# Slot zero of an eight-slot attention and FFN kernel: VectorE's additions, a low part, and the row sums' way through DRAM in another order

## What is computed

```
xn  = layernorm(x)
t, p, g = Wt @ c,  Wp @ xn,  Wg @ c            # 512x512 by 512x2048
att = sum over a group of p * g                 # 8 groups of 64 channels
y   = group-norm( Wz_grouped @ (att * t) ) * gn_w + gn_b
x1  = x + y + c
x2  = layernorm(x1)
out = x1 + FFN(x2[:, perm]) un-permuted         # 16 heads: 128 -> 512 -> gelu -> 128
```

## Time and profile before

| | |
|---|---|
| median of 3 runs | 1519.7 us (1517.99, 1519.7, 1523.19) |
| span of the profiled execution, first to last instruction | 1516.6 us |
| lowest run, beside that span | 1517.99 us, 1.4 us above it |
| PE busy | 1496.1 us, 99% of the span |
| DVE, ACT, POOL busy | 1192.4, 1065.8, 962.8 us |
| slot zero's S products, y products, v products start at | 5.2, 55.3, 100.6 us |

### The profile page before, as it was taken

The page is one execution under the profiler, slowest core; times in us unless marked ns, Lnnn a source line. Parts: engine busy times, 40 slices in busy tenths (PEclk is TensorE's granted clock), DMA queues, the critical chain, the costliest instruction groups (busy, mean ns, idle before and its releaser), DMA issues.

```text
span 1516.6 us, 19144 instructions
## 1 busy us (share of the span) xinstructions
PE 1496.1 (99%) x6592; PEld 1233.7 (81%) x6592; DVE 1192.4 (79%) x1514; ACT 1065.8 (70%) x1321; POOL 962.8 (63%) x765
## 2 busy tenths in 40 slices
PE   8999999998999999999999999999999999999998
PEld 7878888887888888888888888888888888777886
DVE  4989868875788767887678877888778876889876
ACT  4636757844878568784687847878378773899876
POOL 1673686297862668626784357834579355898887
PEclk9999999999999999999999999999999999999999
DMA  9998788786677936778376784767747776768886
GB/s 327 330 379 332 229 301 298 269 265 204 202 264 266 276 118 221 246 262 278 119 237 248 246 260 133 261 237 250 231 146 275 249 237 204 236 197 257 289 285 221
DMA packets 166865, 374.76 MB, mean 247 GB/s; under 512 B 14960, under 2 KB 80496, under 8 KB 158576
## 3 DMA queue, kind: packets, MB, share of 16 engines
q1 hardware_dynamic: 141424, 281.25, 56.3%
q0 software_dynamic: 25344, 92.29, 17.3%
HBM read 287.45 MB, written 86.03 MB: 246 GB/s over the span
## 4 chain that ended last, share of the span: by engine, by line
PE 80%; DVE 4%; POOL 4%; DMA 4%; ACT 3%; issue 3%; SPq 0%; POOLq 0%; ACTq 0%; DVEq 0%
PE PP L892 13%; PE PP L938 12%; PE PP L953 12%; PE PP L896 6%; PE PP L941 6%; PE PP L957 6%; PE PP L879 6%; PE PP L880 6%; PE PP L874 6%; PE PP L909 4%; PE PP L913 2%; POOL out L1346 1%; POOL FB L1338 1%; POOL FB L1341 1%; ACT Z L1031 1%
## 5 line engine op out<-in xcount | busy, mean ns | idle before, releaser
L938 PE MATMUL PP<-GG,WW 128*128 128x512 f32 x1008 | 270.5, 390 | 4.4 <-issue 4.4
L1046 ACT ACTIVATE PP<-PP 128x1024 f32<-128x1024 f32 x256 | 262.0, 1024 | 0.0
L1249 DVE TENSOR_TENSOR R<-PP,R 128x1024 fp32r<-128x1024 f32 x175 | 213.6, 1220 | 52.5 <-ACT PP L1046 50.6
L892 PE MATMUL PP<-R,WC 128*128 128x512 f32 x1024 | 253.1, 389 | 0.7 <-ACT Z L998 0.7
L1330 POOL TENSOR_TENSOR X<-X,RAW 128x512 f32<-128x512 f32 x112 | 189.2, 1725 | 96.4 <-DVE bn L1069 71.6
L1045 ACT ACTIVATE R<-PP 128x1024 fp32r<-128x1024 f32 x175 | 180.1, 1029 | 87.5 <-PE PP L941 86.5
L938 PEld LDWEIGHTS PP<-GG,WW 128*128 128x128 f32 x1008 | 189.6, 188 | 44.4 <-issue 4.8
L892 PEld LDWEIGHTS PP<-R,WC 128*128 128x128 f32 x1024 | 192.1, 188 | 41.0 <-ACT Z L998 1.1
L1084 DVE TENSOR_TENSOR R<-RAW,R 128x1024 fp32r<-128x1024 f32 x128 | 184.1, 1445 | 49.8 <-ACT R L976 49.8
L1346 POOL DMA_INDIRECT out<-FB,perm_sb x128 | 153.4, 1198 | 82.0 <-DVE FB L1255 64.1
L1323 POOL DMA_INDIRECT FB<-xg_scratch,perm_sb x128 | 127.7, 997 | 115.1 <-DMA xg_scratch<-FB 74.4
(11 more groups left out here) (122 smaller groups left out, 2582.5 us busy)
## 6 DMA issues: line engine op xcount, KB each, us to landing
WW<-w_scratch SPq DMA_DIRECT2D x148, 512.0 KB
X<-in_x SPq DMA_DIRECT2D x32, 1024.0 KB, 6.0
RAW<-in_cx SPq DMA_DIRECT2D x32, 1024.0 KB
RAW<-in_xT SPq DMA_DIRECT2D x63, 512.0 KB
RAW<-in_cT SPq DMA_DIRECT2D x63, 512.0 KB
xg_scratch<-FB SPq DMA_DIRECT2D x104, 256.0 KB
w_scratch<-WW POOLq DMA_DIRECT2D x16, 1024.0 KB, 6.8
HX<-wp_scratch SPq DMA_DIRECT2D x7, 1024.0 KB, 8.2
```

The lines of the kernel that those rows point to most:

```text
L892: eng.matmul(PP[2 + ot // 2][:, ot % 2, :], WC[:, l, ct, part(ot)], u[:, ct, :], start=(l == 0 and ct == 0), stop=False)
L938: eng.matmul(pp[:, e, :], wt[:, l, part(2 * p + e)], g[:, 0, :], start=(l == 0), stop=False)
L1046: eng.activation(pp[:], pp[:], ACT.Gelu).then_inc(S["gelu"], 1)
L1249: eng.tensor_tensor(h_tile(f, p, 1), PP[slot["up", f, p]][:], f32(h_tile(f, p, 0)), ALU.subtract).then_inc(S["hlo"], 1)
```

## The change

It touches the table of numbers in `plan()`, for slot zero (`first`) and at one place slot one, and moves two stages of slot zero from SP's list to ACT's.

```diff
@@ -602,12 +602,12 @@
             put(t + 0.2, s_lo, i, dt)
             for c1 in range(NT):
                 whole = i < 2 or dt > 3
-                put(s0 + (dt + 0.08 * c1 if whole else S_EARLY[c1 // 2][dt][c1 % 2]), s_hh, i, dt, c1)
+                put(s0 + (0.81 if (i, dt, c1) == (1, 0, NT - 1) else dt + 0.08 * c1 if whole else S_EARLY[c1 // 2][dt][c1 % 2]), s_hh, i, dt, c1)
                 put(s0 + (dt + 0.34 + 0.16 * c1 if whole else S_EARLY[c1 // 2][dt][c1 % 2]), s_mm, i, dt, c1)
         for q in range(NQ):
             for ct in range(NT):
                 t = s0 + 6 + 2.1 * ct + 0.4 * q + (1.9 if ct == 3 else 0)
-                t = 10.4 + 1.4 * ct + 0.22 * q if first else s0 + 11 + 2.1 * ct + 0.5 * q if i == 1 else t
+                t = (10.4, 12.65, 14.05, 15.0)[ct] + (0.22 if ct < 3 else 0.15) * q if first else s0 + 11 + 2.1 * ct + 0.5 * q if i == 1 else t
                 put(t, bn_x, i, ct, q)
         if first:
             for ct in range(NT):
@@ -619,14 +619,15 @@
         put(y0 + (12.4 if 0 < i < 3 else 4.2), load_wg, i)
         for q, t in enumerate((y0 - 3, y0 + 0.4, y0 + 4.3, y0 + 8.3)):
             put(t, y_hi, i, q)
-            put(t + 0.2, y_lo, i, q)
+            put(y0 - 0.2 if first and q == 1 else t + 0.2, y_lo, i, q)
         for q, t in enumerate((y0 - 1, y0 + 1.2, y0 + 2.6, y0 + 4.6)):
             for ct in range(NT):
                 put(t + 0.25 * ct + late, row_c, i, q, ct)
-                put(y0 - 1.5 + 2.4 * q + 0.5 * ct + 2 * late, add_c, i, q, ct)
+                tc = (y0 - 2.1, y0 - 2.05, y0 - 1.2, y0 - 0.4)[ct] if q == 0 else y0 + (0.9, 4.6, 6.4)[q - 1] + 0.5 * ct
+                put(tc if first else y0 - 1.5 + 2.4 * q + 0.5 * ct + 2 * late, add_c, i, q, ct)
         put(y0 + 5.8 + late, sum_c, i)
         put(y0 + 5.9 + late, store_sum, i)
-        put(y0 + 7.6 + late, spread_sum, i)
+        put(y0 + (10.5 if first else 7.6 + late), spread_sum, i)
         for c1 in range(NT):
             put(y0 + 11.3 + (0.6 if i < 2 else 0) + 0.6 * c1, s_fix, i, c1)
             put(y0 + 11.5 + (0.6 if i < 2 else 0) + 0.6 * c1, s_evh, i, c1)
@@ -648,9 +649,9 @@
         put(v0 + 3.4, aggr_y, i)
         put(f0 + 1.2, g_mean_mm, i)
         put(f0 + 1.25, g_mean, i)
-        put(f0 + 2.3, g_var_mm, i)
-        put(f0 + 2.35, g_var_a, i)
-        put(f0 + 2.4, g_root, i)
+        put(f0 + (3.3 if first else 2.3), g_var_mm, i)
+        put(f0 + (3.35 if first else 2.35), g_var_a, i)
+        put(f0 + (3.4 if first else 2.4), g_root, i)
         put(f0 + (3.9 if first else 5.25), g_var_b, i)
 
 
@@ -1045,6 +1046,19 @@
                 eng.activation(h_tile(f, p, 0), pp[:], ACT.Gelu).then_inc(S["hhi"], 1)
                 eng.activation(pp[:], pp[:], ACT.Gelu).then_inc(S["gelu"], 1)
 
+            elif stage == "store_sum" and a[0] == 0:
+                i = a[0]
+                act.wait_ge(*at["sst", i, "row"])
+                for r in range(4):
+                    eng.dma_start(vs_d[i].rearrange("(t r j) -> t r j", r=4, j=32)[:, r, :],
+                                  rowc[32 * r:32 * r + NT, :]).then_inc(S["vs"], 16)
+            elif stage == "spread_sum" and a[0] == 0:
+                i = a[0]
+                act.wait_ge(*at["vs", i])
+                for t in free["sb", i]:
+                    act.wait_ge(*t)
+                eng.dma_start(FB[:, SBT, :], vs_d[i].partition_broadcast(P)).then_inc(S["sbt"], 16)
+
     def vector(eng):
         dve = Passed(eng, S)
         for stage, *a in order:
@@ -1426,13 +1440,13 @@
                 sp.wait_ge(*at["wk", h])
                 eng.dma_start(f32(w_tile(w)[:, 2 * j:2 * j + 2, :]), w_d[h, :, 2 * j:2 * j + 2, :]).then_inc(
                     S[f"w{w if w in (2, 3) else w % 2}{j}"], 16)
-            elif stage == "store_sum":
+            elif stage == "store_sum" and a[0]:
                 i = a[0]
                 sp.wait_ge(*at["sst", i, "row"])
                 for r in range(4):
                     eng.dma_start(vs_d[i].rearrange("(t r j) -> t r j", r=4, j=32)[:, r, :],
                                   rowc[32 * r:32 * r + NT, :]).then_inc(S["vs"], 16)
-            elif stage == "spread_sum":
+            elif stage == "spread_sum" and a[0]:
                 i = a[0]
                 sp.wait_ge(*at["vs", i])
                 for t in free["sb", i]:
```

## The result

| | before | after |
|---|---|---|
| median (runs) | 1519.05 us (1513.31 to 1528.01, 20) | 1525.3 us (1521.19 to 1531.47, 20) |
| ratio, 95% interval | | 1.0039 [1.0026, 1.0052] |
| span of the profiled execution | 1516.6 us | 1519.5 us |

The median rose by 6.25 us, against the 4.9 forecast, and stands at 1525.3 us, against the forecast of 1524.6. Executions of one kernel lie up to 15 us apart (1513.31 to 1528.01 us before), so one span says little by itself.

The account below looks back on a forecast made before the run. PE, busy 1496.1 of 1516.6 us, was taken as the bound. Hold 5.4, less stall 1.37 and moves 0.4, plus clock 1.3, gives 4.9; 1519.7 + 4.9 = 1524.6 us, range 1519.5 to 1529.

Parts of the forecast that it names:

- The hold on ACT: Slot zero: ACT's stores wait for DVE's transposed row, holding chunk one's copies; PE begins chunk two 5.4 us later.
- The low part's stall: Chunk two in slot zero: PE's stall for DVE's low part goes for certain, worth 1.37 us.
- The last addition: DVE's last addition before the row sums: free of POOL's issues, row at 80.5; held by them, 81.4.
- The clock: Behind PE's idle time before chunk two, the clock falls to half, as near 351 us: 1.3 us lost.
- The sum to the v products: Slot zero's v products: PE comes 4.9 us later than its former 100.60, at 105.5.
- 0.4 us for the two moves by one unit: Between 93 and 119 us: two moves and what the second tiny matmul waits give PE back 0.4 us.
- rival 3: Slot zero's read back lands late, 11 us instead of 6.2; v products 2.7 us later, 1527 to 1529; chance 0.12.
- the cover: Before slot zero's v products: the read back's chain has 2.1 us to spare; landings over 8.3 us delay PE.
- I take that one to be paced by PE itself, since its gathers and buffers follow: PE's 4.4 us wait near 351 us follows tiles PE has finished, so the shift from slot zero stays.

Follow-up runs that it names:

- e2: Changed kernel with slot zero's row-sum stores still on ACT but behind both copies and chunk three's high part: 1519.39 us, ratio 0.9999 to the kernel before.
- e3: Changed kernel with slot zero's row sums on DVE earlier, y0 + 4.55 instead of y0 + 5.8: 1522.77 us, ratio 1.0006 to the kernel before.
- e5: Kernel before with only slot zero's row-sum stores and read back moved to ACT's list, DVE's order old: 1528.06 us, ratio 1.0066.
- b2: The kernel before, unchanged, run and profiled a second time: 1518.52 us, ratio 1.0008.
- e4: Changed kernel with 24 repeated matmuls in chunk one's last y tile to keep PE busy while it waits: 1521.94 us, ratio 1.0016 to the kernel before.
- e6: Kernel before with only the two late moves by one unit, slot one's high-by-high product and the second tiny matmul with what follows: 1517.43 us, ratio 0.9998.
- a2: The changed kernel, unaltered, run and profiled a second time: 1524.22 us, ratio 1.0042 to the kernel before.
- e1: Changed kernel with the row sums' stores and read back returned to SP's list, numbers unaltered: 1523.42 us, ratio 1.0024 to the kernel before.

## Why the prediction was right, point by point

- **The hold on ACT.** As forecast: a row at 79.57 (80.5), four issues of 1.52 us (1.3), and PE at 82.23 (82.9), 4.76 us late instead of 5.4. The 0.9 us at the row are all in its start: DVE got to chunk two's low part at 71.53, after waiting 1.23 us for ACT's high part, and not at 72.50, and from there the row took 8.0 us, as forecast. POOL's cast moved with DVE, from 74.23 to 71.94. e2 shows that the order is all of it: a gain of 6.4 us at the first anchor with the same issues on ACT; e3, the changed kernel and e5, with rows at 75.3, 79.6 and 83.0, give steps of PE of 0.9, 5.7 and 8.4 us.
- **The low part's stall.** It went, as forecast; its price before, 1.37 us, came back as 1.4 in b2.
- **The last addition.** Two estimates stood against each other, a row at 80.5 and at 81.4. The addition at 78.58 took 0.67 us while POOL issued transfers at 78.35 and 78.89. In this place it went by what the Trainium skill, SBUF — State Buffer, "Who interferes with whom", infers, that writing a transfer's descriptors does not hold such an addition. The 1.52 us of the earlier trace rows beside such an issue stay unexplained.
- **The clock.** 1.3 us forecast, 1.6 measured between the changed kernel and e4. The idle time was 5.3 us, longer than the 4.4 from which the term was taken.
- **The sum to the v products.** The terms that act ahead of them are 5.4 - 1.37 + 1.3 = 5.3 us, and PE was 5.2 late (105.77 against 100.60). The hold was 0.6 us smaller and the clock 0.3 dearer, so the closeness is partly luck. The prediction's own 105.5 had already taken off 0.4 us for the two moves, which act only behind this point.
- **The term that was mis-sized: 0.4 us for the two moves by one unit.** In the kernel before the moves take away waits of 0.8 us (e6). In the changed kernel they bring nothing, since a new wait of 1.2 us (0.6 in a2) stands there. From the first v product to the first anchor it is 15.77 us where it was 14.84, so 5.2 us late become 6.1. The median rose by 6.25.
- **The read back as a second bound (rival 3).** It landed 8.7 us after its issue, where 6.2 was forecast and 8.3 was the limit of the cover. But the issue came at 89.65 and not at 91.1, beside ACT's copy and not behind it, so the landing was at 98.3, and ACT's last row of S ended at 104.4, 1.4 us ahead of PE's 105.77. The rival did not happen in the changed kernel, but it is what e1 and e2 ran into as soon as the hold was gone.
- **"I take that one to be paced by PE itself, since its gathers and buffers follow"**. This was wrong. The gather waits for POOL, and POOL for its own stores to land, so the wait is not fixed: it differs by 7 us between the two profiles of the changed kernel and by 2 between those of the kernel before. The shift did stay in the medians. The wait's short turn, with the clock kept, is why the profiled span rose by 2.9 us only, while the second anchor moved by 5.5. A single pair of spans would have put the change at half its size.

No variant beats the kernel before beyond its interval. The best, e2 and e6, are at 0.9999 and 0.9998.

## What to carry to other kernels

A transfer that is issued from a compute engine's list makes everything behind it on that list wait for what the transfer waits for: 6.79 us of ACT's time here, 10.56 in e5. Its price is the producer's real lateness at that place, not its own 0.4 us; put it behind the work that others wait for, as in e2. Before a stall is worth removing, look for the next chain that ends just behind it: here the chain through DRAM and slot one's load of c had next to no cover, and took each gain back in turn. And compare two profiles stage by stage at fixed anchors, not by their spans, since one wait that varies between executions can hide the whole change.

## What the runs showed of the hardware

- Four stores of 0.5 KB need 1.5 us of issue on ACT, and 1.9 in e3; their read back of 256 KB landed 6.4 us after its issue in e4, 6.5 in e2, 7.9 in e1 and 8.7 in the changed kernel.
- The clock fell to half behind waits of PE of 1.9 us (e1), 2.5 (b2), 4.4 (before), 5.3 (changed), 8.0 (e5) and 9.7 (a2). It stayed at 1.00 behind waits of 1.9 us at e2's v products and of 2.7 us near 350 us in the changed kernel, so the length of the wait alone does not tell. In e4, where PE was kept busy through the wait, it stayed at 1.00.
- A copy of 4 numbers per partition on DVE took 2.22 us beside POOL's low part, as long as an addition of 128x512 beside one (2.26). Away from it they take 0.44 and 0.67 us.
